# Squares of Wv and Wo summed on ScalarE instead of Gram products on TensorE, with another order of blocks in steps 0 to 7

## The reference, cut to what matters

```python
x = x + xattn(layernorm(x), ctx, Wq, Wk, Wv, Wo, gq, gk)   # 16 batches of 128x256; 16 heads of 128
x = x + ffn(layernorm(x), w_gate, w_up, w_down, ln_weight)
# xattn, for each batch:
q = rmsnorm(h @ Wq) ; k = rmsnorm(ctx @ Wk) ; v = ctx @ Wv     # rmsnorm over the 128 of a head
p = softmax(q @ k.T / sqrt(128))
return (p @ v) @ Wo
# ffn: activations rounded to 8 bits by row, weights to {-1, 0, 1} by their mean absolute value
```

## Time and profile before

| | us |
|---|---|
| median of 3 runs | 471.62 (471.61 to 473.48) |
| the profiled execution's own time | 473.02 |
| its span in the trace | 470.9 |
| busy PE / PEld | 413.0 / 319.4 |
| busy DVE / ACT / POOL | 430.5 / 428.6 / 391.1 |

### The profile page before, as it was taken

One profiled execution on the slowest core, in us unless ns is written; L12 is line 12 of the kernel. 1 busy time (PEld: TensorE's weight loads), 2 busy tenths in 40 slices (PEclk: granted clock), 3 DMA queues, 4 the chain that ended last, 5 costly groups with the idle time before them and its releaser, 6 DMA issues.

```text
span 470.9 us, 14733 instructions
## 1 busy us (share of the span) xinstructions
PE 413.0 (88%) x4554; PEld 319.4 (68%) x4554; DVE 430.5 (91%) x1249; ACT 428.6 (91%) x1454; POOL 391.1 (83%) x362
## 2 busy tenths in 40 slices
PE   0399867889999999999999999999999679789886
PEld 0388654777787777777777787777777455556555
DVE  3789899899999999999999999999898868999995
ACT  3488899999999999999999999999999679999982
POOL 2034958799999999999999999999999966888882
PEclk9999999999999999999999999999999999999998
DMA  8941824265354354354354354354466541001001
GB/s 292 431 170 24 307 51 91 59 121 137 89 118 106 89 114 109 89 117 106 89 114 109 89 120 103 90 116 108 92 102 105 133 68 24 13 22 36 22 33 57
DMA packets 140238, 50.18 MB, mean 107 GB/s; under 512 B 135856, under 2 KB 137904, under 8 KB 139312
## 3 DMA queue, kind: packets, MB, share of 16 engines
q1 hardware_dynamic: 139920, 48.78, 41.9%
q10 hardware_dynamic: 288, 1.05, 0.6%
HBM read 14.16 MB, written 2.10 MB: 35 GB/s over the span
## 4 chain that ended last, share of the span: by engine, by line
ACT 28%; POOL 27%; issue 20%; DVE 14%; PE 6%; DMA 3%; POOLq 1%; SPq 0%; DVEq 0%; ACTq 0%
ACT work L706 10%; POOL rkq L553 8%; POOL work L543 6%; POOL phl L565 6%; ACT kjunk L744 5%; ACT qshl L728 4%; POOL qshl L530 3%; ACT qhl L638 3%; DVE ham L1241 3%; ACT work L730 2%; ACT ohl L755 2%; DMA stage<-in_wqP 2%; POOL stage L607 1%; POOL hrr L613 1%; DMA kT<-khl 1%
## 5 line engine op out<-in xcount | busy, mean ns | idle before, releaser
L706 ACT ACTIVATE work<-SO,nbias,rkq 128x128 f32<-128x128 f32 x256 | 115.9, 483 | 2.2 <-DVE nbias L1080 2.1
L553 POOL TENSOR_TENSOR rkq<-kqe,negh 128x8 f32<-128x8 f32 x65 | 109.7, 1688 | 4.2 <-DVE kqe L1067 3.7
L381 PE MATMUL KQ<-hT,wqs 128*128 (+1 forms) x1536 | 99.3, 221 | 8.7 <-DVE wqs L929 6.7
L381 PEld LDWEIGHTS KQ<-hT,wqs 128*128 128x128 f16 x1536 | 91.9, 99 | 14.4 <-issue 11.7
L381 PE MATMUL EB<-As,ohl 128*128 128x256 f16 x768 | 94.3, 273 | 0.4 <-issue 0.4
L530 POOL TENSOR_TENSOR qshl<-work,qshl 128x512 f16<-128x512 f32 x64 | 74.6, 1165 | 23.5 <-ACT work L730 23.5
L381 PEld LDWEIGHTS EB<-As,ohl 128*128 128x128 f16 x768 | 75.1, 98 | 22.7 <-issue 0.8
L565 POOL TENSOR_TENSOR phl<-work,phl 128x512 f16<-128x512 f32 x64 | 74.1, 1158 | 12.2 <-DVE phl L1151 10.4
L543 POOL TENSOR_TENSOR work<-work,rinv 128x512 f32<-128x512 f32 x64 | 66.7, 1041 | 4.6 <-DVE rinv L1025 4.6
L381 PEld LDWEIGHTS SO<-kT,qhl 128*128 128x128 f16 x768 | 44.5, 98 | 28.8 <-DMA kT<-khl 18.6
L381 PE MATMUL SO<-kT,qhl 128*128 128x128 f16 x768 | 53.5, 219 | 9.0 <-DMA kT<-khl 5.0
(11 more groups left out here) (164 smaller groups left out, 937.6 us busy)
## 6 DMA issues: line engine op xcount, KB each, us to landing
xs<-in_xP SPq DMA_DIRECT2D x4, 512.0 KB, 21.0
stage<-in_wqP SPq DMA_DIRECT2D x4, 512.0 KB, 10.6
wvo<-in_woP SPq DMA_DIRECT2D x1, 2048.0 KB, 17.9
out<-wqs SPq DMA_DIRECT2D x16, 128.0 KB, 1.7
raw<-in_ctxT ACTq DMA_DIRECT2D x1, 1024.0 KB, 6.5
wvo<-in_wvP SPq DMA_DIRECT2D x1, 1024.0 KB, 13.5
raw<-in_ctxP SPq DMA_DIRECT2D x1, 1024.0 KB, 19.9
kT<-khl SPq DMA_TRANSPOSE x64, 2.8
```

Source lines behind the costliest of these rows:

```text
L381: last = matmul(out, lhsT=left(i), rhs=right(j), start=start and n == 0, stop=stop and n == 2)
L553: pool.tensor_tensor(rkq[:, g % 4, :], kqe[:, g % 2, :], negh[:, 0:2 * HG], ALU.pow).then_inc(root_ok, 1)
L706: ins = act.activation(pe[:, s, c], SB[:, c], ACT.Exp, scale=rkq[:, (g - AT_X + 1) % 4, HG + h:HG + h + 1], bias=nbias[:, s, h:h + 1], acc ...
```

## The change

The Gram products, the trace on DVE and their semaphores go. In their place ACT squares Wv (one pass, step 0) and Wo (two passes, step 1), each pass 128x2048 float32, with a running sum into a column of `ssA`; the squares themselves are written into `As`, which is free until products A. PE sums three columns instead of two. The scale is made in step 1 instead of 2, and products A start in step 2 instead of 3. The lists of `fill` and `early` are in another order on all four engines, and the tables place the set-up work differently. The lists of `step`, `drain` and `ffn` are as they were.

```diff
-A_AT = {3: (0, 4), 4: (4, 6), 5: (6, 8)}
-TOT_AT = 2
-SQ_AT = {0: (0, 2), 1: (2, 4), 2: (4, 6)}
-STAT_AT = {1: (1, 2), 2: (2, 3), 3: (3, 4)}
-ROOT_AT = {1: (1, 2), 3: (2, 4)}
-APPLY_AT = {0: (2, 4), 2: (4, 8), 4: (8, 12), 6: (12, 16)}
-LN_AT = {'first': (0, 1), 0: (1, 2), 2: (2, 3), 3: (3, 4), 4: (4, 5), 5: (5, 6), 6: (6, 8)}
-C_AT = {2: (0, 1), 3: (1, 4)}
+A_AT = {2: (0, 2), 3: (2, 4), 4: (4, 6), 5: (6, 8)}
+TOT_AT = 1
+SQ_AT = {0: (0, 1), 1: (1, 3)}
+STAT_AT = {0: (1, 2), 1: (2, 4)}
+ROOT_AT = {1: (1, 2), 2: (2, 4)}
+APPLY_AT = {0: (2, 4), 1: (4, 8), 3: (8, 12), 4: (12, 14), 5: (14, 16)}
+LN_AT = {'first': (0, 1), 1: (1, 2), 2: (2, 3), 3: (3, 4), 4: (4, 5), 5: (5, 6), 6: (6, 8)}
+C_AT = {1: (0, 1), 2: (1, 2), 3: (2, 3), 4: (3, 4)}
...
-        HI_AT = {'start': (0, 3), 1: (3, 9), 2: (9, 11), 4: (11, 12)}
-        LO_AT = {'start': (0, 1, 2), 0: (3, 4, 5, 6, 7), 1: (8,), 5: (9, 10), 6: (11,)}
+        HI_AT = {'start': (0, 3), 0: (3, 9), 1: (9, 10), 2: (10, 12)}
+        LO_AT = {'start': (0, 1, 2), 0: (3, 4, 5, 6), 1: (7,), 2: (8,), 5: (9,), 6: (10, 11)}
...
+            def A_squares(at):
+                for i in range(*SQ_AT.get(at, (0, 0))):
+                    act.wait_ge(wvo_in[0 if i else 1], 16)
+                    src = wo_f[:, H // 2 * i - H // 2:H // 2 * i, :] if i else wvT_f
+                    act.activation(As[:, i % 2, H // 2 * (i // 2):H // 2 * (i // 2) + H // 2, :].rearrange("p h n -> p (h n)"),
+                                   src.rearrange("p h c -> p (h c)"), ACT.Square,
+                                   accum_out=ssA[:, i:i + 1]).then_inc(sumA_ok, 1)
...
-            def gram_trace(b, g):
...
-            def grams(at):
...
-                    te.wait_ge(sumA_ok, 1)
+                    te.wait_ge(sumA_ok, 3)
                     te.wait_ge(qse_ok, TOT_AT)
-                    te.matmul(MB[:, 4:6], lhsT=ones_f[:, :], rhs=ssA[:, :], start=True, stop=True).then_inc(totA_ps, 1)
+                    for c, i in ((4, 0), (5, 1), (5, 2)):
+                        ins = te.matmul(MB[:, c:c + 1], lhsT=ones_f[:, :], rhs=ssA[:, i:i + 1],
+                                        start=i < 2, stop=i != 1)
+                    ins.then_inc(totA_ps, 1)
```

More of the change, by code:

```diff
@@ L124, in build_program @@
         scl = sb("scl", [P, 6])
-        ssA = sb("ssA", [P, 2])
+        ssA = sb("ssA", [P, 3])
         nrmA = sb("nrmA", [P, 2])
@@ L207, in build_program @@
         A_ps = sem("A_ps")
-        gram_ps = sem("gram_ps")
-        gram_ok = sem("gram_ok")
         sumA_ok = sem("sumA_ok")
@@ L568, in fill @@
             def fill(b, g):
+                roots_at(b, g)
+                q_square_low(b, g)
                 A_root(b, g)
-                q_square_low(b, g)
                 c_lows(b, g)
-                roots_at(b, g)
                 kq_roots(b, g)
             def early(b, g):
-                c_lows(b, g)
                 q_square_low(b, g)
@@ L579, in early @@
                 p_scaled(b, g)
+                A_root(b, g)
                 p_low(b, g)
-                A_root(b, g)
                 kq_roots(b, g)
+                c_lows(b, g)
             def step(b, g):
@@ L679, in A_out @@
                     act.wait_ge(A_ps, i + 1)
+                    act.wait_ge(sumA_ok, 3)
                     act.wait_ge(Ascl_ok, 1)
@@ L686, in ln_highs, with A_squares_at @@
                     ln_high(now(b, g) - 1)
+            def A_squares_at(b, g):
+                A_squares(now(b, g))
             def c_highs(b, g):
@@ L757, in fill @@
             def fill(b, g):
+                A_squares_at(b, g)
+                ln_highs(b, g)
+                splits_at(b, g)
+                q_pieces(b, g)
+                c_highs(b, g)
                 ffn_absolutes(b, g)
[L759 to L762, removed]
                 k_squares(b, g)
@@ L767, in early @@
                 ln_highs(b, g)
-                splits_at(b, g)
[L769 to L775, removed]
+                exponentials(b, g)
+                A_squares_at(b, g)
+                q_pieces(b, g)
+                c_highs(b, g)
+                ffn_absolutes(b, g)
+                o_high(b, g)
+                k_squares(b, g)
+                A_outs(b, g)
+                splits_at(b, g)
             def step(b, g):
@@ L1161, in fill, with early @@
             def fill(b, g):
+                q_norm(b, g)
+                row_max(b, g)
+                ln_lows(b, g)
+                splits_at(b, g)
                 statistics_at(b, g)
-                ln_lows(b, g)
[L1164 to L1170, removed]
+                A_total_in(b, g)
+                q_low(b, g)
+                k_high(b, g)
+                biases(b, g)
+                k_low(b, g)
+                A_lows(b, g)
+                k_norm(b, g)
+                layernorms(b, g)
+                A_scale(b, g)
+            def early(b, g):
+                x1_stats(b, g)
+                splits_at(b, g)
+                ln_lows(b, g)
+                p_sums(b, g)
+                psum_consts(b, g)
+                A_scale(b, g)
                 k_high(b, g)
-                k_norm(b, g)
-                A_total_in(b, g)
                 k_low(b, g)
[L1175 to L1182, removed]
                 layernorms(b, g)
                 p_reciprocal(b, g)
-                A_scale(b, g)
-                splits_at(b, g)
-                ln_lows(b, g)
+                q_low(b, g)
+                q_norm(b, g)
+                row_max(b, g)
+                ffn_scales(b, g)
                 statistics_at(b, g)
-                q_low(b, g)
-                row_max(b, g)
-                psum_consts(b, g)
+                p_high(b, g)
                 biases(b, g)
-                k_high(b, g)
+                k_norm(b, g)
                 A_lows(b, g)
+                o_low(b, g)
+                A_total_in(b, g)
                 residual(b, g)
[L1196 to L1201, removed]
             def step(b, g):
@@ L1413, in scores @@
                     s, r = (g - AT_S) % 2, (g - AT_S) % 4
-                    if now(b, g) == AT_S:
-                        te.wait_ge(sumA_ok, 1)
                     need_dma(te, kT_in[s], b, g, AT_S)
@@ L1445, in ln_transposed @@
                 ln_transposes(now(b, g) if now(b, g) >= 0 else None)
-            def grams_at(b, g):
-                grams(now(b, g))
             def A_total(b, g):
                 if now(b, g) == TOT_AT:
-                    te.wait_ge(sumA_ok, 1)
+                    te.wait_ge(sumA_ok, 3)
                     te.wait_ge(qse_ok, TOT_AT)
-                    te.matmul(MB[:, 4:6], lhsT=ones_f[:, :], rhs=ssA[:, :], start=True, stop=True).then_inc(totA_ps, 1)
+                    for c, i in ((4, 0), (5, 1), (5, 2)):
+                        ins = te.matmul(MB[:, c:c + 1], lhsT=ones_f[:, :], rhs=ssA[:, i:i + 1],
+                                        start=i < 2, stop=i != 1)
+                    ins.then_inc(totA_ps, 1)
                     for s in wvo_in:
@@ L1475, in fill @@
             def fill(b, g):
+                second_maxima(b, g)
+                q_sums(b, g)
                 q_product(b, g)
                 scores(b, g)
-                second_maxima(b, g)
-                q_sums(b, g)
                 k_product(b, g)
                 A_products(b, g)
-                grams_at(b, g)
                 A_total(b, g)
@@ L1486, in early @@
             def early(b, g):
+                k_product(b, g)
                 q_product(b, g)
-                q_sums(b, g)
+                second_maxima(b, g)
                 A_products(b, g)
                 output(b, g)
+                A_total(b, g)
+                q_sums(b, g)
+                e_product(b, g)
+                ln_transposed(b, g)
                 scores(b, g)
[L1492 to L1497, removed]
                 ffn_sums(b, g)
```

## The result

The changed kernel takes 470.37 us (median of 22 runs, 468.85 to 474.68), the kernel before 472.23 (22 runs, 471.21 to 473.48). The ratio is 0.9971, 95% interval [0.9958, 0.9984]: -1.4 us, clear of its own uncertainty but under the 0.5% that I had set. The forecast was 470.1, a change of -1.5. Run once more on another occasion the same kernel gave 0.9989 [0.9968, 1.0010], which is not told from no change. The changed kernel scatters more than the old one: 5.8 us from its fastest to its slowest run, against 2.3.

What follows compares the result with a forecast made beforehand. Steps 0 to 7 were bounded by nearly full DVE and ACT; the loop has no slack. Entry -1.0 and first loop turns -0.5 gave -1.5 us: 471.5 profiled, 470.1 as median, forecast 469.2 to 471.3, whole range 467.8 to 473.6.

Steps and rivals of the forecast that it cites:

- its layout of the queues: Hand-made timetable of the four engines' new lists for steps 0 to 8, keeping 0.5 us of ACT idle.
- its own signs of being wrong: ACT idle over 2 us from 23.3 to loop; q products of steps 3-7 over 2 us; four loop steps not 20.1.
- worth what ACT and DVE waited for them: Steps 0 to 3: removing Gram products, some 13 us of PE's queue, gains only the waits they caused, not 13 us.
- the entry: ACT's arrival at the loop after step 7: forecast 1.0 us earlier, from 1.8 at most less remaining idle and gaps.
- by the rows nothing is lost there: Steps 1 and 2: q products slowed to 2.7 us by PE's clock are covered by ACT's squares, costing nothing.
- The rival of the slow pace: PE stays at half pace from step 3's q product (45.4): +5 us once, 475.1; chance 0.07.
- The prediction's own reading, from the stretch of 70 to 75: PE busy 2.28 of 5 us, next q product still 1.50: a warm array stays warm at that load.
- The loop's first turn: Steps 8 to 12 took 21.1 us against 20.1 later; 0.5 of that 1.0 us, range 0 to 1.0, forecast as gain.
- "ACT is full": Rival: no ACT idle before the loop (1.8) and the first turns' whole 1.0 gained: -2.8 us, 468.8; chance 0.17.
- DVE's order: Rival: `q_low(1)` behind statistics and late `k_norm` in steps 2 and 3; two 1 us misses give 472.1; chance 0.2.

Runs made afterwards that it cites:

- The added matmuls: 23 additional float32 matmuls of Wv blocks on PE in steps 0 to 2, added to the changed kernel; ratio to the kernel before 0.9991, loop entry 81.56.
- The four bn_stats more: The changed kernel with one chunk of layernorm statistics done twice by DVE in step 1; ratio to the kernel before 0.9970, loop entry 84.06.
- the third pass: The changed kernel with one more square pass of Wo on ACT in step 1; ratio to the kernel before 0.9994, loop entry 82.88.
- the late maxima: The changed kernel with second maxima behind PE's q product of step 0, as before the change; ratio to the kernel before 1.0015, loop entry 83.40.
- two other kernels with the old lists: The kernel before with Gram products and trace replaced by three square passes, ratio 1.0049; or left out with the norms, ratio 1.0007.

## Why the prediction was right

*Right in its reading of where the room is, and in its layout of the queues up to step 2.* Squares at 17.9, 30.8 and 32.7 (said: 18, about 31 and 33), each 1.9 us; scales 23.3; q products of steps 0, 1 and 2 at 22.6, 31.4 and 38.4 (22.7, 31.0, 38.2). ACT had no idle in step 1. Of its own signs of being wrong one came true, though by little: ACT has 2.1 us of idle from 23.3 to the loop, where over 2 was to count against it, and ACT's L696 stands at 83.5 and not at 82 to 83.

*Right in where the Gram products stood in the way, wrong in weighing it:* "worth what ACT and DVE waited for them". They also kept PE at 2.4 GHz. In the old order that was worth more at the entry than what they cost: 84.80 without them, 83.65 with, by one profile each.

*The step that was mis-sized is "by the rows nothing is lost there".* I let the longer q products of steps 1 and 2 be covered by ACT's passes, and so they were. I left out the products A, which the change had moved into step 2. They ran at up to double the time, +1.0 and +0.7 us, and ACT waited for 2.0 us where I had 0.5. So the entry came 0.2 us early instead of 1.0. The rival of the slow pace had its place one step too late (products of step 3, from 45.4): the clock came back at 46, and so its +5 us did not come. The rule of the Trainium skill (TensorE: Matmul & The Clock Gate, section "HAM oscillation — how this bites in real kernels") that idle stretches put the array back to the lower clock agrees with the first fall: PE stood from 26.2 to 30.6, and the clock was at 0.50 from about 29. The second fall, at about 39.3, came with no pause of PE over 1.0 us since 36; it is the one that made products A slow, and no rule that I had gives it. The prediction's own reading, from the stretch of 70 to 75, that a warm array stays so with little to do did not carry over to it.

*The loop's first turn* (+0.5 us gained by the forecast, 0 to 1.0) gave 0.8 in one profile and cost 0.6 in the other. The median of 22 runs has both kinds in it. That the forecast met the ratio is thus partly luck: in the profiled pair the entry gave 0.2 us instead of 1.0, the first turn 0.8 instead of 0.5, and the rest of loop and tail 0.9, for which the forecast had nothing. The 470.1 itself was reckoned from 471.62, a median of three runs where the 22 have 472.23, so that the change is the better measure of it than the time.

*"ACT is full" (rival, -2.8)* could not come with PE at half clock. With it up, entry reached 81.6, as that rival had it. But the time then stayed at 0.9991, so in that run an earlier entry was no earlier end. The added matmuls may have a part in this: the instruction packets on q8 around the entry come at 82.0 and 90.7 with them instead of 84.9 and 97.1. That wasn't tested. *DVE's order* (about no change) did bind, but as the layout had it and without its misses of 1 us: DVE reached `q_low(1)` at 37.54 (said: 37.35), when ACT had the high part at 36.87. The four bn_stats more show it: they went through to the first product A in full.

*What stays open.* Whether the instruction loads are what makes single transposes land 1.5 us late. In the kernel before, seven of their packets lie between 70 and 110, two between 110 and 320, eleven between 320 and 400, the same stretches as the late landings, and every late one has a packet within it. That speaks for a collision between the two, but no run moved the loads. How much of the 0.1 to 0.3% is due to the change of order and how much to where these packets fall is open too, and so is what makes the clock fall in step 2.

## What to carry to other kernels

Work on PE that "only fills its queue" may be what keeps its clock; before taking it away, look at what PE does in the steps behind it, and which product on the path comes first there. An experiment that moves PE's work can also move its clock: compare kernels at the same pace, or a delay and a faster product cancel and both look like slack, as the third pass and the late maxima did here. An order of queues and a split of work between engines are one change: each alone can lose what both together win. And a gain at the end of the set-up is worth something only if the loop behind it takes it on: read the first turn and the tail as well as the entry.

## What the runs showed of the hardware

- In the changed kernel the granted clock fell to 0.50 at about 29, with PE idle since 26.2. It was at 1.00 from 35.9, when PE had been busy since 31.4, fell again at about 39.3 and rose at 46.1. In the second profile of the same kernel that second fall came only at 43, with PE idle for the 2 us before it. The first q product, at 22.6, ran at half pace (2.74 us) with the column at 1.00, as that of step 0 did before the change (2.72 against 1.50 later, with 1.00 throughout): a 1.00 at the start of a trace does not say that PE runs at 2.4 GHz.
- A kernel that enters its loop within 0.3 us of itself can end 3.5 us apart. The spread of single runs of the changed kernel (468.7 to 474.7) is larger than the effect under study, and even ratios over 12 to 22 runs differ by 0.2% from one occasion to the next.
- A transposing DMA of k lands 2.7 to 2.8 us after its issue as a rule. All eighteen that took 4.0 to 4.9 us had a packet of an instruction queue begin while they were under way.
- On DVE, the last operation of the second scales took 0.53 us before the change, ending within 0.05 us of a POOL operation (24.30 to 25.45), and 0.17 after it, with POOL idle. In the two other kernels with the old lists it took 0.73 and again ended with the POOL operation; with late maxima and POOL idle, 0.17. Nothing was changed to test it.
